# Second attention on one Trainium2 core: q and k in two float32r parts instead of three bf16 parts, heads of even and odd number on separate partition halves

## The chip, the core and the metric

The kernel runs on one core of a Trainium2 chip. A core has a matrix engine (TensorE, in the views PE for its matmuls and PEld for the loading of their stationary operands), a vector engine (DVE), an engine for activations (ACT), a general one (POOL) and one that issues transfers (SP). They run side by side and wait for each other with semaphores. The metric is the device time of one execution in microseconds, lower is better; the time of a version is the median of its runs.

## The reference

Two layers are computed on 2048 tokens of 128 features: a windowed attention, a memory layer, a second attention and a layer of experts, each behind a layer norm. The change is in the second attention: 16 heads of width 8 over one sequence of N = 2048.

```python
def _L1_attn_ref(x, Wq, bq, Wk, bk, Wv, bv, Wo, bo):
    ...
    q = (x @ Wq.T + bq).reshape(B, N, H, d).transpose(0, 2, 1, 3)
    k = (x @ Wk.T + bk).reshape(B, N, H, d).transpose(0, 2, 1, 3)
    v = (x @ Wv.T + bv).reshape(B, N, H, d).transpose(0, 2, 1, 3)
    q, k = _rope(q, k)
    scores = jnp.einsum('bhnd,bhmd->bhnm', q, k) / jnp.sqrt(jnp.asarray(d, x.dtype))
    attn = jax.nn.softmax(scores, axis=-1)
    out = jnp.einsum('bhnm,bhmd->bhnd', attn, v)
```

## The kernel before

The kernel is written engine by engine, with every wait by hand. Four stages take nearly all the time: the first attention (until about 400 us of the span), the memory layer (until about 480), the second attention with its projections (482 to 1376), and the experts (the last 90 us).

`project1_block` makes q and k with their rotation, 512 columns at a time in eight jobs, and splits each float32 value into three bf16 parts whose sum is the value. DVE rotates and takes the first rest, ACT rounds, POOL takes the last rest (line 847), and SP stores the parts to device memory.

`attn1_block` then works through the 16 heads. For one head, all scores of a query with 2048 keys are needed twice:

- **R**, the row-maximum matmuls (`rows`, line 973): queries on the output's partitions, keys along the free axis, 64 matmuls of 128 by 512 per head. DVE takes the maximum of 1024 columns at a time (line 1055), so 32 reductions per head.
- **E**, the exponential's matmuls (line 1019): keys on the partitions, queries along the free axis, again 64 of 128 by 512. The maximum of each query is subtracted inside the matmul by extra contraction rows, which hold the negated maxima in parts. ACT takes the exponential of each (line 1127).
- **AV** (`weigh`, line 999): values and a column of ones, in float32, weighted by the exponentials. The four blocks of 512 queries stand side by side on four strips of 32 columns of the array. A float32 matmul is two instructions in the views.

A head has 16 *slots* t of 128 keys (numbered 0 to 15 here). In slot t, TensorE issues four E, E0 to E3, with R of a later head between them, and then AV of slot t - 1. Each E waits for a free bank: two banks hold scores for ACT, so E2 waits for the exponential of E0 and E3 for that of E1. R starts 12 matmuls ahead (`LEAD`), so in slots 0 to 12 R belongs to head h + 1 and in slots 13 to 15 to head h + 2. At the end of slot 13 `turn_max` (line 982) turns the maxima of the next head, DVE copies them (line 1076), and SP writes them into the contraction rows. After slot 15 DVE copies the sums (line 1082), TensorE turns them, and DVE divides.

Heads 0 to 11 run in a hardware loop of four rounds with three heads each; heads 12 to 15 are written out. Between E the loop places R by this line:

```python
for c, beside in enumerate((1, 2, 1, 0)):
```

so nothing stands between E3 and AV. q and k of a head are one tile of 72 or 75 partitions (three parts times three parts times eight, and three rows for the maximum).

Of the kernel before, what the change touches and what calls it, by code (L numbers as in the profile page):

```python
# [6 lines left out]
F32 = mybir.dt.float32  # L7
BF16 = mybir.dt.bfloat16
U32 = mybir.dt.uint32
ACT = mybir.ActivationFunctionType  # L10
ALU = mybir.AluOpType
# [23 lines left out]
PARTS = 3  # L35
QROWS = PARTS * PARTS * HD1
MROW = QROWS
KROWS = QROWS + PARTS
VCOLS = 32
# [717 lines left out]
def project1_block(nc, m, a):  # L757

    with ExitStack() as ctx:
# [9 lines left out]
        rot = sb("rot", [P, 2, BANK])  # L769
        rest = sb("rest", [P, 2, BANK])  # L770
        parts = sb("parts", [P, 2, PARTS, N], BF16)

        swapped = sem("swapped")
        qk_ready, partner_ready = sem("qk_ready"), sem("partner_ready")
        rot_ready, part1, rest_ready, part2, part3 = sem("rot_ready"), sem("part1"), sem("rest_ready"), sem("part2"), sem("part3")
# [28 lines left out]
        def _(dve):  # L804
# [5 lines left out]
            for s in range(JOBS + 1):  # L810
                if s < JOBS:
                    u, i, c = s, s // NC, s % NC
                    dve.wait_ge(qk_ready, u + 1)
                    if u >= 2:
                        dve.wait_ge(rot_ready, u - 1)
                    cols = slice(c * BANK, (c + 1) * BANK)
                    nc.vector.scalar_tensor_tensor(direct[:, u % 2, :], m.psum[:, 2 * (u % 3), :], biases[i][:, 0:1],
                                                   m.cos[:, cols], ALU.add, ALU.mult)
                    nc.vector.scalar_tensor_tensor(partner[:, u % 2, :], m.psum[:, 2 * (u % 3) + 1, :], biases_sw[i][:, 0:1],
                                                   m.sin[:, cols], ALU.add, ALU.mult).then_inc(partner_ready, 1)  # L820
                u = s - 1
                if u >= 0:
                    i, c = u // NC, u % NC
                    dve.wait_ge(rot_ready, u + 1)
                    dve.wait_ge(part1, u + 1)
                    if u >= 2:
                        dve.wait_ge(part3, u - 1)
                    nc.vector.tensor_tensor(rest[:, u % 2, :], rot[:, u % 2, :], parts[:, i, 0, c * BANK:(c + 1) * BANK],
                                            ALU.subtract).then_inc(rest_ready, 1)
                if s < JOBS:  # L830
                    dve.wait_ge(partner_ready, s + 1)
                    if s >= 2:
                        dve.wait_ge(rest_ready, s - 1)
                    nc.vector.tensor_tensor(rot[:, s % 2, :], direct[:, s % 2, :], partner[:, s % 2, :], ALU.add).then_inc(rot_ready, 1)
# [5 lines left out]

        @block.gpsimd
        def _(pool):
            for u in range(JOBS):
                i, c = u // NC, u % NC
                pool.wait_ge(part2, u + 1)
                cols = slice(c * BANK, (c + 1) * BANK)
                nc.gpsimd.tensor_tensor(parts[:, i, 2, cols], rest[:, u % 2, :], parts[:, i, 1, cols], ALU.subtract).then_inc(part3, 1)

        @block.scalar
        def _(act):  # L850
            for s in range(JOBS + 1):
                if s < JOBS:
                    i, c = s // NC, s % NC
                    act.wait_ge(rot_ready, s + 1)
                    nc.scalar.activation(parts[:, i, 0, c * BANK:(c + 1) * BANK], rot[:, s % 2, :], ACT.Copy).then_inc(part1, 1)
                u = s - 1
                if u >= 0:
                    i, c = u // NC, u % NC
                    act.wait_ge(rest_ready, u + 1)
                    nc.scalar.activation(parts[:, i, 1, c * BANK:(c + 1) * BANK], rest[:, u % 2, :], ACT.Copy).then_inc(part2, 1)  # L860

        @block.sync
        def _(sp):
            for u in range(JOBS):
                i, c = u // NC, u % NC
                cols = slice(c * BANK, (c + 1) * BANK)
                sp.wait_ge(part3, u + 1)

                sp.dma_start((m.q_parts, m.k_parts)[i].rearrange("s r n -> r s n")[:, :, cols], parts[:, i, :, cols]).then_inc(stored, 16)
            sp.wait_ge(stored, 16 * JOBS)  # L870


def attn1_block(nc, m, a):

    SCALE = HD1 ** -0.5
    HALF = 2 * BANK  # L880
    NB = 3
    with ExitStack() as ctx:
# [6 lines left out]
        qf = sb("qf", [KROWS, NB, N], BF16)  # L889
        kf = sb("kf", [KROWS, NB, N], BF16)  # L890
        vx = sb("vx", [P, NB, NT, VCOLS])
        pb = sb("pb", [P, 2, NC, BANK])
        rowmax = sb("rowmax", [P, NT, 2])
        nmax = sb("nmax1", [P, NT])
        nrest = sb("nrest", [P, NT])
        nparts = sb("nparts", [P, P // NT, NT], BF16)
        nT = sb("nT", [PARTS * NT, P], BF16)
# [3 lines left out]
        loaded = [sem(f"qk_loaded{b}") for b in range(NB)]  # L901
        ones_loaded = sem("ones_loaded")
        nparts_zeroed = sem("nparts_zeroed")
        vx_zeroed, vx_ready = sem("vx_zeroed"), sem("vx_ready")
        rows_ready, rows_reduced = sem("rows_ready"), sem("rows_reduced")
        nmax_ready, npart1, nrest1, npart2, npart3 = sem("nmax_ready"), sem("npart1"), sem("nrest1"), sem("npart2"), sem("npart3")
# [5 lines left out]

        START = 2

        def start_counts(eng, *sems):
            for s in sems:
                eng.sem_inc(s, START)


# [3 lines left out]
        ROUNDS = H1 // NB - 1  # L923
        LEAD = 12
        LOAD = 16 * 2 * PARTS

# [5 lines left out]
        def _(sp):  # L932
            def load(h, b):
# [7 lines left out]
            def max_rows(g, b):  # L941

                sp.wait_ge(nT_saved, START + g + 1)
                sp.dma_start(qf[QROWS:KROWS, b, :], nT[:, :]).then_inc(max_rows_loaded, 16)

            for b in range(NB):
                load(b, b)
                if b == 0:
                    sp.dma_start(kf[QROWS:KROWS, :, :], m.ones_rows.rearrange("r (o n) -> r o n", o=1)
                                 .broadcast_to([PARTS, NB, N])).then_inc(ones_loaded, 16)  # L950
            max_rows(0, 0)
            with sp.Fori(0, ROUNDS) as r:
                for b in range(NB):
                    max_rows(r * NB + b + 1, (b + 1) % NB)

                    sp.wait_ge(av_done, START + (r * NB + b + 1) * NT)
                    load(r * NB + b + NB, b)
            for h in range(H1 - 1 - NB, H1 - 1):
                max_rows(h + 1, (h + 1) % NB)
                if h == H1 - 1 - NB:  # L960
                    sp.wait_ge(av_done, START + (h + 1) * NT)
                    load(h + NB, h % NB)
# [538 lines left out]
```

## Time and profile before

| what | value |
|---|---|
| median of 3 runs | 1500.69 us (1499.51 to 1502.81) |
| span of the profiled execution | 1493.4 us |
| its mean granted TensorE clock | 0.939 of full speed |
| TensorE busy | 1353.5 us (91%) |
| DVE busy | 1035.1 us (69%) |
| ACT busy | 916.2 us (61%) |
| POOL busy | 173.4 us (12%) |

The span runs from the first to the last instruction. The profiled execution has no separate time of its own beside it; the median of the runs is 7.3 us above its span, and this is taken as what lies around the span. Busy shares are averages over stages with different limits, and a busy TensorE is not one at its peak.

### The profile page before, as it was taken

Reading aid. Unit: us, or ns where it says so; the run is one execution under the profiler, and the core shown is the slowest. Engines: PE = TensorE matmul, PEld = TensorE weight load, DVE = VectorE, ACT = ScalarE, POOL = GpSimd, SP = SyncE. Lnnn points to the kernel's source line nnn. Section 1 sums busy time; section 2 is a strip of 40 time slices with the busy share of each in tenths; the row PEclk is TensorE's granted clock in tenths of the full one; section 3 lists DMA queues with packets and bytes.
Section 4 is the critical chain, followed back from the end, with each engine's and each line's share of the span. In section 5 each row is a group of like instructions: output and inputs, shape, how many; then the busy total and the mean of one; then the engine's idle time right before and its main releaser. Section 6 shows DMA issues by size and latency. Waiting matters only on the chain. (4 is left out here: it accounts for less than half of the span.)

```text
span 1493.4 us, 24477 instructions
## 1 busy us (share of the span) xinstructions
PE 1353.5 (91%) x7460; PEld 605.9 (41%) x7460; DVE 1035.1 (69%) x1993; ACT 916.2 (61%) x2409; POOL 173.4 (12%) x321
## 2 busy tenths in 40 slices
PE   4999999999787669999899989998999999999698
PEld 2676776777545301222222222222222222223466
DVE  4677777777768678888677877887788887750400
ACT  2666666666565303776577667666766676668442
POOL 3233222333320500000000000000000000001200
PEclk8899999999989755999799989999999999999799
DMA  3100000000000210000000000000000000000200
GB/s 84 49 8 9 5 2 8 7 2 1 1 1 1 87 46 1 5 13 17 18 1 17 17 18 1 17 17 11 8 17 17 2 16 17 1 1 1 49 0 28
DMA packets 21889, 23.33 MB, mean 16 GB/s; under 512 B 5640, under 2 KB 18184, under 8 KB 21522
## 3 DMA queue, kind: packets, MB, share of 16 engines
q1 hardware_dynamic: 21778, 21.94, 4.5%
q8 instruction: 58, 0.95, 0.3%
q14 instruction: 53, 0.43, 0.1%
HBM read 17.54 MB, written 4.19 MB: 15 GB/s over the span
## 5 line engine op out<-in xcount | busy, mean ns | idle before, releaser
L1127 ACT ACTIVATE pb<-psum 128x512 f32<-128x512 f32 x1024 | 554.1, 595 | 288.3 <-PE psum L1019 287.6
L1055 DVE TENSOR_REDUCE rowmax<-psum 128x1 f32<-128x1024 f32 x512 | 602.9, 1219 | 147.7 <-PE psum L973 147.2
L1019 PE MATMUL psum<-qf,kf 75*128 75x512 bf16 x1024 | 395.0, 394 | 14.6 <-issue 10.0
L973 PE MATMUL psum<-kf,qf 72*128 72x512 bf16 x1024 | 374.8, 408 | 31.2 <-DVE rowmax L1055 16.7
L999 PE MATMUL psum<-pb,vx 128*32 128x512 f32 x2048 | 274.8, 614 | 0.6 <-ACT pb L1127 0.6
L1019 PEld LDWEIGHTS psum<-qf,kf 75*128 75x128 bf16 x1024 | 99.2, 98 | 391.0 <-ACT pb L1127 331.1
L490 ACT ACTIVATE pr<-sm,nmax 128x128 f32<-128x128 f32 x256 | 100.7, 394 | 104.6 <-DVE nmax L429 101.9
L973 PEld LDWEIGHTS psum<-kf,qf 72*128 72x128 bf16 x1024 | 99.6, 100 | 137.7 <-DVE rowmax L1055 63.5
L527 POOL TENSOR_TENSOR pr<-pr,rtotal 128x256 f32<-128x256 f32 (+1 forms) x256 | 110.5, 453 | 262.9 <-DVE rtotal L437 262.9
L424 DVE TENSOR_TENSOR sm<-psum,mask 128x320 f32<-128x320 f32 x128 | 62.2, 486 | 48.4 <-PE psum L298 48.4
L298 PE MATMUL psum<-kx,qz 128*128 128x160 f32 x512 | 92.1, 303 | 0.0
L298 PEld LDWEIGHTS psum<-kx,qz 128*128 128x128 f32 x512 | 79.0, 193 | 28.0 <-issue 27.7
L1144 POOL COPY vx<-v 128x128 f32 (+1 forms) x16 | 4.6, 293 | 716.6 <-PE psum L999 716.6
L492 ACT ACTIVATE pr<-sm,nmax 128x32 f32<-128x32 f32 x256 | 78.3, 306 | 0.0
L999 PEld LDWEIGHTS psum<-pb,vx 128*32 128x32 f32 x2048 | 42.0, 108 | 73.8 <-issue 61.5
L338 PE MATMUL psum<-wo_cur,oT 128*128 128x128 f32 x256 | 62.8, 327 | 0.2
L325 PE MATMUL psum<-pt,gv 64*128 64x128 f32 x256 | 62.7, 325 | 0.0
L1323 ACT ACTIVATE hT<-psum,b 128x512 f32<-128x512 f32 x48 | 33.0, 687 | 43.2 <-PE psum L1338 43.0
L428 DVE TENSOR_REDUCE nmax<-sm 128x2 f32<-128x256 f32 x128 | 53.8, 420 | 4.4
L327 PE MATMUL psum<-pt,v 128*64 128x128 f32 x512 | 56.7, 300 | 0.0
L312 PE MATMUL psum<-ident,pr 128*128 128x128 f32 x256 | 51.0, 281 | 5.6 <-POOL pr L527 4.4
L443 DVE COPY pt<-psum 128x256 f32<-128x256 f32 x128 | 50.8, 397 | 1.5 <-PE psum L314 1.3
(198 smaller groups left out, 1337.7 us busy)
## 6 DMA issues: line engine op xcount, KB each, us to landing
qf<-q_parts SPq DMA_DIRECT2D x48, 96.0 KB
kf<-k_parts SPq DMA_DIRECT2D x48, 96.0 KB
q_parts<-parts SPq DMA_DIRECT2D x4, 384.0 KB, 2.5
k_parts<-parts SPq DMA_DIRECT2D x4, 384.0 KB, 2.5
cos<-cos_table SPq DMA_DIRECT2D x1, 1024.0 KB, 5.2
sin<-sin_table SPq DMA_DIRECT2D x1, 1024.0 KB, 7.0
out<-x SPq DMA_DIRECT2D x1, 1024.0 KB, 5.1
w_cur<-in_L_attn_wq SPq DMA_DIRECT2D x8, 64.0 KB, 1.9
```

Of the source, the lines that this page charges most:

```text
L298: mm = nc.tensor.matmul(m.psum[:, S_B + i % 2, j * WL:(j + 1) * WL], qz[:, b, j, s * P:(s + 1) * P], kx[:, b, s, :], start=True, stop=True)
L325: nc.tensor.matmul(ob, gv[:, b, :], pt[0:2 * G0, w % 2, 2 * P:3 * P], start=True, stop=False)
L338: nc.tensor.matmul(m.psum[:, Y_B, (w % TPB) * P:(w % TPB + 1) * P], oT[:, w % 4, :], wo_cur[:, b, :], start=True, stop=True).then_inc(wo_d ...
L424: nc.vector.tensor_tensor(sm[:, i % 4, :], m.psum[:, S_B + i % 2, 0:2 * WL], m.mask[:, :], ALU.add).then_inc(masked, 1)
L490: nc.scalar.activation(pr[:, i % 4, j * P:(j + 1) * P], sm[:, i % 4, j * WL:j * WL + P], ACT.Exp, bias=nmax[:, i % 4, j:j + 1], accum_out= ...
L492: mm = nc.scalar.activation(pr[:, i % 4, 2 * P + j * G0:2 * P + (j + 1) * G0], sm[:, i % 4, j * WL + P:(j + 1) * WL], ACT.Exp, bias=nmax[: ...
L527: mm = nc.gpsimd.tensor_tensor(prw, prw, rb, ALU.mult)
L973: mm = nc.tensor.matmul(m.psum[:, M_B + (u % 2) * 2 + n % 2, :], qf[0:QROWS, b, t * P:(t + 1) * P], kf[0:QROWS, b, c * BANK:(c + 1) * BANK ...
L999: mm = nc.tensor.matmul(m.psum[c * VCOLS:(c + 1) * VCOLS, A_B, :], vx[:, b, t, :], pb[:, t % 2, c, :], start=(t == 0), stop=(t == NT - 1))
L1019: nc.tensor.matmul(m.psum[:, bank, :], kf[:, b, t * P:(t + 1) * P], qf[:, b, c * BANK:(c + 1) * BANK], start=True, stop=True).then_inc(st_ ...
L1055: nc.vector.tensor_reduce(rowmax[:, u // 2, u % 2:u % 2 + 1], m.psum[:, M_B + (u % 2) * 2:M_B + (u % 2) * 2 + 2, :].rearrange("p b c -> p ...
L1127: nc.scalar.activation(pb[:, t % 2, c, :], m.psum[:, exp_bank(k, last)[0], :], ACT.Exp, scale=SCALE).then_inc(exp_ready, 1)
```

## The change

q and k are split into two float32r parts instead of three bf16 parts. (float32r is a float32 of which the matrix engine uses a shortened mantissa.) A head then needs 33 contraction rows for R and 35 for E: even heads are held on partitions 0 to 63, odd ones on 64 to 127. E of head h and R of head h + 1 lie on different halves of the array's rows. The order on TensorE becomes one R behind each E, and all 16 heads are written out. In `project1_block` DVE and ACT each lose a step of the split, and POOL's now reads the rotated value itself. On DVE the split of the maxima falls away; it is done behind the transpose, in two steps instead of one copy. POOL fills the constant rows, which a transfer did before.

```diff
-PARTS = 3
-QROWS = PARTS * PARTS * HD1
-MROW = QROWS
+PARTS = 2
+PROWS = PARTS * PARTS * HD1
+QROWS = PROWS + 1
 KROWS = QROWS + PARTS
+HALFP = P // 2
 VCOLS = 32
...
-                    nc.vector.tensor_tensor(rest[:, u % 2, :], rot[:, u % 2, :], parts[:, i, 0, c * BANK:(c + 1) * BANK],
-                                            ALU.subtract).then_inc(rest_ready, 1)
...
+                nc.scalar.activation(parts[:, i, 0, c * BANK:(c + 1) * BANK], rot[:, u % 3, :], ACT.Copy).then_inc(high_ready, 1)
...
+                nc.gpsimd.tensor_tensor(parts[:, i, 1, cols], rot[:, u % 3, :], parts[:, i, 0, cols].bitcast(F32),
+                                        ALU.subtract).then_inc(low_ready, 1)
...
-        qf = sb("qf", [KROWS, NB, N], BF16)
-        kf = sb("kf", [KROWS, NB, N], BF16)
+        qf = sb("qf", [P, SLOTS, N], F32R)
+        kf = sb("kf", [P, SLOTS, N], F32R)
...
+        def group(h):
+            return h % 2 * HALFP
+        def slot(h):
+            return h // 2 % SLOTS
...
+            def load(h):
+                g0, b = group(h), slot(h)
+                hd = slice(h * HD1, (h + 1) * HD1)
                 for j in range(PARTS):
-                    rows = slice(j * PARTS * HD1, (j + 1) * PARTS * HD1)
-                    k = m.k_parts[j, bass.ds(h * HD1, HD1), :].rearrange("(o d) n -> o d n", o=1)
-                    sp.dma_start(qf[rows, b, :], m.q_parts[:, bass.ds(h * HD1, HD1), :]).then_inc(loaded[b], 16)
-                    sp.dma_start(kf[rows, b, :], k.broadcast_to([PARTS, HD1, N])).then_inc(loaded[b], 16)
+                    part = slice(g0 + j * PARTS * HD1, g0 + (j + 1) * PARTS * HD1)
+                    q = m.q_parts[j, hd, :].rearrange("(o d) n -> o d n", o=1).broadcast_to([PARTS, HD1, N])
+                    sp.dma_start(qf[part, b, :].bitcast(F32), q).then_inc(loaded[h % 4], 16)
+                    sp.dma_start(kf[part, b, :].bitcast(F32), m.k_parts[:, hd, :]).then_inc(loaded[h % 4], 16)
+            def max_rows(h):
+                g0, b = group(h), slot(h)
+                sp.wait_ge(nT_saved, h + 1)
+                sp.dma_start(qf[g0 + QROWS:g0 + QROWS + 1, b, :].bitcast(F32), nT[0:NT, :].bitcast(F32)).then_inc(max_rows_loaded, 16)
+                sp.dma_start(qf[g0 + QROWS + 1:g0 + KROWS, b, :].bitcast(F32), nT[HALFP // 2:HALFP // 2 + NT, :].bitcast(F32)).then_inc(max_rows_loaded, 16)
...
+            def rows(g, n):
                 t, c, u = n // NC, n % NC, n // 2
-                if n % 2 == 0:
-                    pe.wait_ge(rows_reduced, START + g * HALVES + u - 1)
-                mm = nc.tensor.matmul(m.psum[:, M_B + (u % 2) * 2 + n % 2, :], qf[0:QROWS, b, t * P:(t + 1) * P],
-                                      kf[0:QROWS, b, c * BANK:(c + 1) * BANK], start=True, stop=True)
+                g0, b = group(g), slot(g)
+                if n % 2 == 0 and g * HALVES + u >= 2:
+                    pe.wait_ge(rows_reduced, g * HALVES + u - 1)
+                mm = nc.tensor.matmul(m.psum[:, M_B + (u % 2) * 2 + n % 2, :], qf[g0:g0 + QROWS, b, t * P:(t + 1) * P],
+                                      kf[g0:g0 + QROWS, b, c * BANK:(c + 1) * BANK], start=True, stop=True)
...
+                nc.tensor.transpose(m.psum[0:2 * NT, T_B, 0:P], nmax[:, :], m.ident[:, :]).then_inc(nT_ready, 1)
...
+            def head(h):
+                g0, b = group(h), slot(h)
+                left = H1 - 1 - h
+                pe.wait_ge(max_rows_loaded, (h + 1) * 32)
                 n = LEAD
                 for t in range(NT + 1):
                     if n == UNITS and left >= 2:
-                        b2 = b + 2
-                        pe.wait_ge(loaded[b2 % NB], r * LOAD + (1 + b2 // NB) * LOAD)
-                    for c, beside in enumerate((1, 2, 1, 0)):
+                        pe.wait_ge(loaded[(h + 2) % 4], ((h + 2) // 4 + 1) * LOAD)
+                    for c in range(NC):
                         if t == NT:
                             break
                         k = t * NC + c
                         bank, banks = exp_bank(k, left == 0)
-                        pe.wait_ge(exp_ready, START + h * UNITS + k + 1 - banks)
-                        nc.tensor.matmul(m.psum[:, bank, :], kf[:, b, t * P:(t + 1) * P],
-                                         qf[:, b, c * BANK:(c + 1) * BANK], start=True, stop=True).then_inc(st_ready, 1)
-                        for _ in range(beside):
-                            if n < UNITS and left >= 1:
-                                rows(h + 1, (b + 1) % NB, n)
-                            elif n >= UNITS and left >= 2:
-                                rows(h + 2, (b + 2) % NB, n - UNITS)
-                            n += 1
+                        if h * UNITS + k + 1 - banks > 0:
+                            pe.wait_ge(exp_ready, h * UNITS + k + 1 - banks)
+                        nc.tensor.matmul(m.psum[:, bank, :], kf[g0:g0 + KROWS, b, t * P:(t + 1) * P],
+                                         qf[g0:g0 + KROWS, b, c * BANK:(c + 1) * BANK], start=True, stop=True).then_inc(st_ready, 1)
+                        if n < UNITS and left >= 1:
+                            rows(h + 1, n)
+                        elif n >= UNITS and left >= 2:
+                            rows(h + 2, n - UNITS)
+                        n += 1
...
+            for h in range(H1):
+                head(h)
...
-            def split_maxima(g):
-                dve.wait_ge(rows_reduced, START + (g + 1) * HALVES)
-                nc.vector.tensor_reduce(nmax[:, :], rowmax[:, :, :], AX_X, ALU.max, negate=True).then_inc(nmax_ready, 1)
-                nc.vector.tensor_copy(nparts[:, 0, :], nmax[:, :]).then_inc(npart1, 1)
-                nc.vector.tensor_tensor(nrest[:, :], nmax[:, :], nparts[:, 0, :], ALU.subtract).then_inc(nrest1, 1)
-                nc.vector.tensor_copy(nparts[:, 1, :], nrest[:, :]).then_inc(npart2, 1)
-                nc.vector.tensor_tensor(nparts[:, 2, :], nrest[:, :], nparts[:, 1, :], ALU.subtract).then_inc(npart3, 1)
+            def save_maxima(g):
+                dve.wait_ge(rows_reduced, (g + 1) * HALVES)
+                nc.vector.tensor_reduce(nmax[:, 0:NT], rowmax[:, g % 2, :, :], AX_X, ALU.max, negate=True).then_inc(nmax_ready, 1)
...
+                nc.vector.tensor_copy(nT[0:NT, :], m.psum[0:NT, T_B, 0:P]).then_inc(nhigh_ready, 1)
+                dve.wait_ge(nhigh_ready, g + 1)
+                nc.vector.tensor_tensor(nT[HALFP // 2:HALFP // 2 + NT, :], m.psum[0:NT, T_B, 0:P], nT[0:NT, :].bitcast(F32),
+                                        ALU.subtract).then_inc(nT_saved, 1)
...
+            for h in range(H1):
                 for k in range(UNITS):
                     t, c = k // NC, k % NC
...
+            for i, g0 in enumerate((0, HALFP)):
+                if i:
+                    pool.wait_ge(edge_rows, 2)
+                nc.gpsimd.memset(qf[g0 + PROWS:g0 + QROWS, :, :].bitcast(F32), 0.0).then_inc(edge_rows, 1)
+                pool.wait_ge(edge_rows, 2 * i + 1)
```

In TensorE's order, here in slot 1 of head 0 (L1019 is E, L973 is R, L999 is AV, the rows of registers are the loop's counts), before:

```order
615 L1019 MATMUL psum<-qf,kf 128x512
616 L972 REGISTER_ALU
617 L973 MATMUL psum<-kf,qf 128x512
618 L1018 REGISTER_ALU
619 L1019 MATMUL psum<-qf,kf 128x512
620 L973 MATMUL psum<-kf,qf 128x512
621 L972 REGISTER_ALU
622 L973 MATMUL psum<-kf,qf 128x512
623 L1018 REGISTER_ALU
624 L1019 MATMUL psum<-qf,kf 128x512
625 L973 MATMUL psum<-kf,qf 128x512
626 L1018 REGISTER_ALU
```

and behind those the fourth E and AV at once:

```order
627 L1019 MATMUL psum<-qf,kf 128x512
628 L999 MATMUL psum<-pb,vx 32x512 x4
629 L1018 REGISTER_ALU
630 L1019 MATMUL psum<-qf,kf 128x512
```

In the changed program the same slot (L992 is E, L945 is R, L972 is AV):

```order
598 L992 MATMUL psum<-qf,kf 128x512
599 L945 MATMUL psum<-kf,qf 128x512
600 L992 MATMUL psum<-qf,kf 128x512
601 L945 MATMUL psum<-kf,qf 128x512
602 L992 MATMUL psum<-qf,kf 128x512
603 L945 MATMUL psum<-kf,qf 128x512
604 L992 MATMUL psum<-qf,kf 128x512
605 L945 MATMUL psum<-kf,qf 128x512
606 L972 MATMUL psum<-pb,vx 32x512 x4
607 L992 MATMUL psum<-qf,kf 128x512
```

The last R has moved from ahead of E3 to between E3 and AV.

On DVE, around the maxima of head 1, before (L1055 is the reduction of R's scores):

```order
746 L1062 TENSOR_REDUCE nmax<-rowmax 128x16
747 L1063 REGISTER_ALU
748 L1064 CAST nparts<-nmax 128x16
749 L1066 TENSOR_TENSOR nrest<-nmax,nparts 128x16
750 L1068 CAST nparts<-nrest 128x16
751 L1070 TENSOR_TENSOR nparts<-nrest,nparts 128x16
752 L1054 REGISTER_ALU
753 L1055 TENSOR_REDUCE rowmax<-psum 128x1
754 L1074 REGISTER_ALU
755 L1076 COPY nT<-psum 48x128
```

and in the changed program (L1023 is the reduction, L1036 and L1038 write the turned maxima):

```order
681 L1030 TENSOR_REDUCE nmax<-rowmax 128x16
682 L1023 TENSOR_REDUCE rowmax<-psum 128x1
683 L1036 CAST nT<-psum 16x128
684 L1038 TENSOR_TENSOR nT<-psum,nT 16x128
685 L1023 TENSOR_REDUCE rowmax<-psum 128x1 x5
```

Four short steps ahead of the transpose are gone, and one has come behind it.

## Rows read from the trace of the kernel before

**Rows 1.** Groups by line: shapes, count | busy us, mean ns | idle before, releaser.

```profile
L1127 ACT ACTIVATE pb<-psum 128x512 f32<-128x512 f32 x1024 | 554.1, 595 | 288.3 <-PE psum L1019 287.6
...
L1055 DVE TENSOR_REDUCE rowmax<-psum 128x1 f32<-128x1024 f32 x512 | 602.9, 1219 | 147.7 <-PE psum L973 147.2
...
L1019 PE MATMUL psum<-qf,kf 75*128 75x512 bf16 x1024 | 395.0, 394 | 14.6 <-issue 10.0 <-ACT pb L1127 3.9
...
L973 PE MATMUL psum<-kf,qf 72*128 72x512 bf16 x1024 | 374.8, 408 | 31.2 <-DVE rowmax L1055 16.7 <-DMA kf<-ones_rows 12.9
```

**Rows 2.** Timeline, one slot of head 4: start us, length us, engine, line.

```profile
802.65 0.39 PE L1019 MATMUL psum<-qf,kf 75*128 75x512 bf16 x1
802.88 0.38 PE L973 MATMUL psum<-kf,qf 72*128 72x512 bf16 x1
...
803.08 2.17 ACT L1127 ACTIVATE pb<-psum 128x512 f32<-128x512 f32 x4 [0.71 <-PE psum L1019]
...
804.22 0.39 PE L1019 MATMUL psum<-qf,kf 75*128 75x512 bf16 x1
804.53 1.07 PE L999 MATMUL psum<-pb,vx 128*32 128x512 f32 x8
805.53 0.39 PE L1019 MATMUL psum<-qf,kf 75*128 75x512 bf16 x1
```

**Rows 3.** Timeline, head 14, slots without row-maximum matmuls.

```profile
1335.82 1.06 PE L999 MATMUL psum<-pb,vx 128*32 128x512 f32 x8
...
1338.77 1.49 PE L999 MATMUL psum<-pb,vx 128*32 128x512 f32 x12
```

**Rows 4.** Timeline, head 12, unrolled, with row-maximum matmuls.

```profile
1215.83 1.06 PE L999 MATMUL psum<-pb,vx 128*32 128x512 f32 x8
...
1218.77 1.07 PE L999 MATMUL psum<-pb,vx 128*32 128x512 f32 x8
```

**Rows 5.** Timeline of TensorE in the first attention.

```profile
302.38 0.38 PE L312 MATMUL psum<-ident,pr 128*128 128x128 f32 x2
302.60 0.27 PE L314 MATMUL psum<-ident,pr 128*64 128x128 f32 x1
302.80 0.49 PE L325 MATMUL psum<-pt,gv 64*128 64x128 f32 x2
```

**Rows 6.** Timeline, slot 14 of head 7.

```profile
982.73 0.22 DVE L1076 COPY nT<-psum 48x128 bf16<-48x128 bf16 x1 [0.58 <-PE psum L982]
...
984.14 0.39 PE L973 MATMUL psum<-kf,qf 72*128 72x512 bf16 x1 [0.76 <-DVE rowmax L1055]
```

**Rows 7.** Timeline: accumulator copies after heads 2, 3, 4; first matmul of head 3.

```profile
728.75 0.69 DVE L1082 COPY acc<-psum 128x512 f32<-128x512 f32 x1 [0.44 <-PE psum L999]
...
733.41 0.61 PE L1019 MATMUL psum<-qf,kf 75*128 75x512 bf16 x1 [3.26 <-issue]
...
787.30 0.69 DVE L1082 COPY acc<-psum 128x512 f32<-128x512 f32 x1 [0.44 <-PE psum L999]
...
836.32 0.69 DVE L1082 COPY acc<-psum 128x512 f32<-128x512 f32 x1 [0.44 <-PE psum L999]
```

**Rows 8.** One stretch: length, busy PE, PEld, DVE, ACT, POOL (count), PEclk (0.50: 1.2 GHz), DMA, GB/s.

```profile
577.00:591.00 14.00, 14.00 (x41) 3.33 (x39) 8.75 (x8) 7.05 (x12) 0.00 (x0) 0.50 0.00 0
```

**Rows 9.** Timeline, head 0, one slot at the low clock.

```profile
583.91 1.93 PE L999 MATMUL psum<-pb,vx 128*32 128x512 f32 x8
...
585.78 0.61 PE L1019 MATMUL psum<-qf,kf 75*128 75x512 bf16 x1
...
586.42 0.60 ACT L1127 ACTIVATE pb<-psum 128x512 f32<-128x512 f32 x1 [1.80 <-PE psum L1019]
...
589.30 1.94 PE L999 MATMUL psum<-pb,vx 128*32 128x512 f32 x8
```

**Rows 10.** Groups by line: one POOL step of the split, one memset.

```profile
L847 POOL TENSOR_TENSOR parts<-rest,parts 128x512 bf16<-128x512 f32 x8 | 16.3, 2048 | 12.2 <-ACT parts L860 12.2
...
L1138 POOL MEMSET vx<- 128x1536 f32 x1 | 1.4, 1377 | 3.4 <-POOLq L759 3.4
```

More of the change, by code:

```diff
@@ L8 @@
 BF16 = mybir.dt.bfloat16
+F32R = mybir.dt.float32r
 U32 = mybir.dt.uint32
@@ L839, in _ @@
                                         m.psum[:, 6 + c % 2, :].rearrange("p (t d) -> p t d", d=D), bv, ALU.add).then_inc(v_saved, 1)
+        @block.scalar
+        def _(act):
+            for u in range(JOBS):
+                i, c = u // NC, u % NC
+                act.wait_ge(rot_ready, u + 1)
+                nc.scalar.activation(parts[:, i, 0, c * BANK:(c + 1) * BANK], rot[:, u % 3, :], ACT.Copy).then_inc(high_ready, 1)
         @block.gpsimd
@@ L844, in _ @@
                 i, c = u // NC, u % NC
-                pool.wait_ge(part2, u + 1)
+                pool.wait_ge(high_ready, u + 1)
                 cols = slice(c * BANK, (c + 1) * BANK)
[L847 to L860, printed above, removed]
+                nc.gpsimd.tensor_tensor(parts[:, i, 1, cols], rot[:, u % 3, :], parts[:, i, 0, cols].bitcast(F32),
+                                        ALU.subtract).then_inc(low_ready, 1)
         @block.sync
@@ L941, in max_rows @@
[L941 to L957, printed above, removed]
@@ L1040, in _ @@
                     turn_max(0)
-                rows(1, 1, n)
-            with pe.Fori(0, ROUNDS) as r:
-                for b in range(NB):
-                    head(r, b)
-            for h in range(ROUNDS * NB, H1):
-                head(h // NB, h % NB)
+                rows(1, n)
+            for h in range(H1):
+                head(h)
         @block.vector
         def _(dve):
-            start_counts(dve, rows_reduced, nmax_ready, npart1, nrest1, npart2, npart3, nT_saved, acc_saved, rsum_ready, att_ready)
@@ L1089, in sums, with maxima @@
                 nc.vector.tensor_tensor(dst, turned[:, :, :, 0:HD1], rb, ALU.mult).then_inc(att_ready, 1)
[L1091 to L1097 removed]
+            def maxima(g):
+                save_maxima(g)
+                if g + 1 < H1:
                     reduce_rows(g + 1, 0, 1)
                 save_turned(g)
[L1100 removed]
+                if g + 1 < H1:
@@ L1101, in maxima @@
                     reduce_rows(g + 1, 1, LEAD // 2)
+            nc.vector.memset(nmax[:, NT:2 * NT], 0.0).then_inc(nmax_zeroed, 1)
+            dve.wait_ge(nmax_zeroed, 1)
             reduce_rows(0, 0, HALVES)
-            maxima(0, True)
-            with dve.Fori(0, ROUNDS) as r:
-                for b in range(NB):
-                    h = r * NB + b
-                    reduce_rows(h + 1, LEAD // 2, HALVES)
-                    maxima(h + 1, True)
-                    sums(h)
-            for h in range(ROUNDS * NB, H1):
+            maxima(0)
```

197 lines of the change are left out of this document (78 added, 119 removed).

## Prediction

> **What bounds the kernel now.** I read the groups by line first, then the timeline of one slot. In the second attention every engine has much to do: ACT 1024 exponentials of 595 ns, DVE 512 reductions of 1219 ns, TensorE 1024 E and 1024 R [rows 1]. Per slot (256 of them) that is 2.4 us of DVE and 2.2 us of ACT. The idle columns matter more: ACT sat idle 287.6 us waiting for E, while TensorE seems never to be idle. That looks like a kernel bound by TensorE, and putting E and R beside each other then looks like a gain of up to 0.4 us a slot, down to DVE's 2.44.
>
> The timeline says otherwise. One slot goes from the E0 at 802.65 to that at 805.53, 2.88 us. It is a chain: E0 to its exponential 0.43 (802.65 to 803.08), two exponentials until E3 may write into the freed bank 1.14 (to 804.22), E3 to AV 0.31 (804.53), AV to the next E0 1.00 (805.53); together 2.88 [rows 2]. R is not in it: R fills gaps. The proof is in head 14, whose last slots have no R at all: AV to AV is still 2.95 us there [rows 3], against 2.94 us in head 12 with four R per slot [rows 4]. So taking R off TensorE's time is worth nothing by itself. What counts is what the change does to the four links of this chain.
>
> The unrolled heads also show a price: 2.94 [rows 4] against 2.88 us in the loop [rows 2]. The loop's ends show another: copy to copy, head 3 takes 58.55 us (728.75 to 787.30), head 4 49.02 (to 836.32); head 3's first matmul came only at 733.41 after 3.26 us of "issue" [rows 7]. The ends of rounds two and three cost 6.8 us each by the same copies (55.8 and 55.7 us), the first 9.5.
>
> **The change part by part.**
>
> *E and R side by side.* As the chain has no R, 0 us in slots 0 to 12, if the halves do run together. The cover is that R3, now between E3 and AV, costs nothing there. Without it R3 adds the step from one matmul to the next, 0.23 us from 802.65 to 802.88 [rows 2]; I take 0.22.
>
> *Loading the stationary operand.* E3 waits for ACT and E0 follows AV, so their weights can't be loaded ahead; the load lies open in the chain twice per slot. For bf16 it shows as almost nothing: the step behind E0 is the same 0.23 [rows 2], hardly more than 512 columns at 2.4 GHz, 0.21. For a four-byte operand the nearest row is the float32 pair at 302.80: two matmuls of 64 rows by 128 columns take 0.49 us together where a pair of transposes takes 0.38, so the open load costs 0.11; the 0.20 from 302.60 to 302.80 against a step of 0.11 is the price of changing the array's shape, 0.09 [rows 5]. That price is paid around AV today as well. Bounds for the load: 0 (as bf16) and 0.11 (as float32). I take 0.10, because float32r has the same 4 bytes and 128 columns, on half the rows, as that row. Thus +0.20 us in each of 13 slots of 15 heads: +39 us.
>
> The Trainium skill, TensorE: Matmul & The Clock Gate, section on weight-path perf modes, says that the fast weight load is on for 128 weights when the dtype is not FP32. Read to the letter, float32r could be fast, which is the first rival below (1494 us); by its other statement, that reading 32 bits at a time brings no win for fp32, the sum stays.
>
> *Slots 13 to 15.* Here R belongs to head h + 2, on the same half as E, so nothing can overlap, and R3 stands in the chain: +0.22, and twice the load, +0.20, in slots 13 and 15. That is 2 x 0.42 x 14 heads = +12 us. Slot 14 is held by DVE today: R waits until 984.14 for a reduction that stood behind the copy at 982.73 [rows 6]. The four short steps that go lay ahead of the transpose, in time in which DVE waited 0.58 us for it anyway; the second step behind it adds some 0.2 us, and E3, still behind R2, is no earlier by more than that. +0.1 x 14 = +1.5 us; bounds -3 and +5.
>
> *Head ends and the last head.* E0 behind the transposes meets a change of shape and an open load, 0.2 x 15 = +3. The last head has no R and four banks; one open load per slot, +1.5.
>
> *Unrolling.* +0.06 us per slot in the 12 heads of the loop, some 14 slots each: +10 us. The ends of the rounds go: 9.5 + 6.8 + 6.8 = -23 us, with the low clock behind them.
>
> *Projections and start.* DVE loses a step, and POOL, with 8 steps of 2048 ns and 12.2 us of idle time in between and before, then sets the pace; each job may get some 0.3 us shorter, -2 to -3. Before the first R, POOL now writes four constant tiles of 4096 columns; at 1377 ns for 1536 columns [rows 10] each takes some 3.5 us, 14 in all, where TensorE waited 12.9 us for the transfer that goes [rows 1]. Nothing to +1. Together -3, bounds -4 and +1. SP issues two transfers for the maxima instead of one, with slots 14 and 15 to hide them before the next head; loads for head h + 4 are queued behind them and are not needed for a whole head. Nothing.
>
> Sum: 39 + 12 + 1.5 + 3 + 1.5 + 10 - 23 - 3 = +41. On the profiled span of 1493.4 that is 1534, and with 7.3 us around the span **1542 us**.
>
> **The rivals.**
>
> *The load is hidden or short (27%).* Then 39 and 1.5 fall away, slots 13 and 15 cost 6, head ends 1.5: -7 us, 1494. At half the price, 1518. For it: that bf16 pays nothing. Against: [rows 5]. This is the rival on the other side; it decides when the open load is under 0.015 us. A version of it in which something in the chain also shortens would go to 1480.
>
> *The low clock spreads (26%).* From 577 to 591, in head 0, TensorE was busy without a gap (14.00 of 14.00 us), E and R with 75 and 72 rows, and the granted clock stayed at 0.50, that is 1.2 GHz [rows 8]. So full busy time did not bring it back at once. The changed kernel does less on TensorE per slot: four pairs and AV are about 1.9 us of 3.1, and from a head's last AV to the first of the next pass some 6 us (an estimate: copy and transposes, then slots 0 and 1). If the clock falls there and does not return before the next end, slots cost what they would at 1.2 GHz. Today such a slot takes 5.39 us (583.91 to 589.30); its AV alone 1.87, E0 to ACT 0.64 [rows 9]. With pairs: 1.87 + 0.8 + 1.14 (ACT does not slow down) + 0.6 = 4.4 to 4.6, so +1.4 over my 3.1. For all 15 heads with their slower ends that is some +350: 1890. If only three slots per head run so, +60: 1600. For it: the work is on 68 rows in two halves, where 75 rows did not suffice. Against: in the loop the clock fell only behind a wait like that of 3.26 us [rows 7], and its mean over the span was 0.939. The same page (Part 1, the HAM clock gate) says that the granted clock has two levels only, half and full; the trace shows no other.
>
> *No overlap (8%).* R3 in the chain of all slots: 0.22 x 13 x 15 = +43 more, 1585. The skill, TensorEngine Tiling (Array Packing), section on key properties, says that tiles run loads and matmuls in parallel. What shows it in this trace is only the four column strips of AV: eight instructions of 614 ns in 1.06 us [rows 2].
>
> *float32r streams its columns twice (5%)*, as each instruction of a float32 pair does: +0.21 in E0 and in E3, about +0.43 x 240 slots = +105: 1645.
>
> *Something shortens the chain (4%)*: 1450 to 1490.
>
> **How the numbers follow.** The forecast itself has 30%, with a range of its own from 1525 to 1560. The likeliest single case is the point, not a mean. Faster by over 0.2% (about what a measurement of this kernel can tell from no change) comes from five sixths of the first rival and the last one, 25%; no change from a price between, 5%; slower from the rest, 70%. The range leaves out the best tenth and the worst: 1487, just under the hidden load, to 1870, just under an attention wholly at the low clock.
>
> **What would show it.** In the changed profile: slots 2 to 12 at 3.14 us from AV to AV, with 0.41 from E3 to AV and 0.53 from E0 to ACT (the load); E and R of a pair starting together; slots 13 and 15 at 3.3 to 3.4; equal head lengths with no "issue" wait of 3 us; granted clock near 1. A slot of 2.94 says that the load was hidden, 3.36 that nothing overlapped, 4.5 with PEclk 0.50 that the clock fell. I am wrong in kind if slots come under 2.88: then TensorE's time did bound, and the slots of head 14 misled me.

## The result and the profile after

The changed kernel takes 1936.2 us (median of 4 runs, 1935.9 to 1938.2), where the kernel before takes 1500.1: the ratio is 1.290, interval 1.288 to 1.292. I had predicted 1542 with a range up to 1870. The profiled execution spans 1933.2 us, 439.8 more than before.

The page of the changed kernel shows where to look (busy tenths in 40 slices, and the granted clock below them):

```profile
PE 1756.5 (91%) x7460; PEld 804.0 (42%) x7460; DVE 1053.8 (55%) x1937; ACT 918.9 (48%) x2398; POOL 181.3 (9%) x325
...
PE   4999999978489999999999999999999999999798
...
PEclk9999999999755555555555555555555555555699
```

DVE and ACT do nearly as much as before in microseconds, but their shares of the longer span have sunk. TensorE looks busy nearly all the time, yet from the eleventh or twelfth slice to the last ones its granted clock is 0.50, that is 1.2 GHz. The groups by line answer to [rows 1]:

```profile
L1082 ACT ACTIVATE pb<-psum 128x512 f32<-128x512 f32 x1024 | 564.8, 596 | 727.4 <-PE psum L992 725.8
L1023 DVE TENSOR_REDUCE rowmax<-psum 128x1 f32<-128x1024 f32 x512 | 625.4, 1225 | 478.1 <-PE psum L945 475.3
L992 PE MATMUL psum<-qf,kf 35*128 35x512 f32 x1024 | 635.4, 703 | 65.1 <-ACT pb L1082 64.7
L945 PE MATMUL psum<-kf,qf 33*128 33x512 f32 x1024 | 630.9, 698 | 19.6 <-POOL kf L1093 15.3
...
L972 PE MATMUL psum<-pb,vx 128*32 128x512 f32 x2048 | 490.5, 1058 | 0.0
```

An exponential takes what it took, but ACT now waits 726 us for E (288 before [rows 1]). AV, which the change did not touch, takes 1058 ns an instruction. One slot of the changed kernel in the timeline (start us, length us), against [rows 2]:

```profile
1003.43 0.79 PE L992 MATMUL psum<-qf,kf 35*128 35x512 f32 x1
...
1003.44 0.79 PE L945 MATMUL psum<-kf,qf 33*128 33x512 f32 x1
...
1004.03 0.62 PE L992 MATMUL psum<-qf,kf 35*128 35x512 f32 x1
1004.03 0.62 PE L945 MATMUL psum<-kf,qf 33*128 33x512 f32 x1
1004.32 1.09 ACT L1082 ACTIVATE pb<-psum 128x512 f32<-128x512 f32 x2 [2.05 <-PE psum L992]
...
1005.56 0.69 PE L992 MATMUL psum<-qf,kf 35*128 35x512 f32 x1
...
1006.18 1.93 PE L972 MATMUL psum<-pb,vx 128*32 128x512 f32 x8
...
1008.05 0.79 PE L992 MATMUL psum<-qf,kf 35*128 35x512 f32 x1
```

The edit does what it says: E and R of a pair start within 0.01 us of each other. But the chain is longer at each link that runs on TensorE: E0 to its exponential 0.89 (0.43 before), E3 to AV 0.62 (0.31), AV to the next E0 1.87 (1.00). Between the exponential and E3, two exponentials on ACT, it is nearly the old one, 1.24 (1.14). Together 4.62 us instead of 2.88. Three stretches of the same trace (length, busy PE, PEld, DVE, ACT, POOL, PEclk, DMA, GB/s) show that the clock stays there:

```profile
612.00:656.00 44.00, 42.09 (x145) 15.46 (x145) 22.23 (x21) 20.19 (x36) 0.00 (x0) 0.50 0.00 1
656.00:662.00 6.00, 4.67 (x28) 1.60 (x20) 3.03 (x5) 1.33 (x3) 0.29 (x1) 0.78 0.04 11
662.00:735.00 73.00, 69.23 (x247) 23.62 (x249) 38.71 (x34) 34.22 (x62) 0.00 (x0) 0.50 0.02 7
```

In head 0 TensorE is busy for 42.09 of 44 us and has the low clock. Only around the end of some heads, behind a slot 15 in which it did AV after AV on all 128 rows, does the full clock come for a few microseconds (the 0.78), and it is gone again within slot 0 of the next head. The accumulator copies, one per head, give the sum. The first row is of the changed kernel, the second of the kernel before (durations, then first and last start):

```profile
L1046 DVE COPY acc<-psum x16: 691/692/692, 658.4 to 1815.2; 128x512 f32<-128x512 f32 x16
```

```profile
L1082 DVE COPY acc<-psum x16: 691/692/692, 630.6 to 1375.2; 128x512 f32<-128x512 f32 x16
```

The first copy is 27.8 us later; the 15 intervals up to the last copy take 1156.8 instead of 744.6 us, +412.2; behind it nothing differs. 27.8 + 412.2 = 440.0, the whole difference of the spans (439.8). All of the loss lies in the second attention and its start: 27.5 us for each interval on the average, and 29 against a head of the loop that has no end of a round (78.1 against 49.0).

### The profile page after: what moved, and what is told of

It is laid out like the page before. It is cut to its first block and busy times, and to the rows that moved or that the text cites. A ratio compares the mean times of both kernels' runs of the same rounds, so it can differ in the third digit from the quotient of the medians.

```text
span 1933.2 us, 21772 instructions
## 1 busy us (share of the span) xinstructions
PE 1756.5 (91%) x7460; PEld 804.0 (42%) x7460; DVE 1053.8 (55%) x1937; ACT 918.9 (48%) x2398; POOL 181.3 (9%) x325
## 5 line engine op out<-in xcount | busy, mean ns | idle before, releaser
L1082 ACT ACTIVATE pb<-psum 128x512 f32<-128x512 f32 x1024 | 564.8, 596 | 727.4 <-PE psum L992 725.8
L1023 DVE TENSOR_REDUCE rowmax<-psum 128x1 f32<-128x1024 f32 x512 | 625.4, 1225 | 478.1 <-PE psum L945 475.3
L992 PE MATMUL psum<-qf,kf 35*128 35x512 f32 x1024 | 635.4, 703 | 65.1 <-ACT pb L1082 64.7
L945 PE MATMUL psum<-kf,qf 33*128 33x512 f32 x1024 | 630.9, 698 | 19.6 <-POOL kf L1093 15.3
L992 PEld LDWEIGHTS psum<-qf,kf 35*128 35x128 f32 x1024 | 276.8, 293 | 625.9 <-issue 330.6
L972 PE MATMUL psum<-pb,vx 128*32 128x512 f32 x2048 | 490.5, 1058 | 0.0
L945 PEld LDWEIGHTS psum<-kf,qf 33*128 33x128 f32 x1024 | 278.4, 297 | 58.3 <-DVE rowmax L1023 31.8
L972 PEld LDWEIGHTS psum<-pb,vx 128*32 128x32 f32 x2048 | 54.6, 142 | 137.7 <-issue 89.8
L1102 POOL COPY vx<-v 128x128 f32<-128x128 f32 x16 | 4.6, 293 | 1060.4 <-PE psum L972 1060.4
L1046 DVE COPY acc<-psum 128x512 f32<-128x512 f32 x16 | 11.1, 692 | 103.4 <-PE psum L972 103.4
```

The lines of the kernel that those rows point to most:

```text
L945: mm = nc.tensor.matmul(m.psum[:, M_B + (u % 2) * 2 + n % 2, :], qf[g0:g0 + QROWS, b, t * P:(t + 1) * P], kf[g0:g0 + QROWS, b, c * BANK:(c ...
L972: mm = nc.tensor.matmul(m.psum[c * VCOLS:(c + 1) * VCOLS, A_B, :], vx[:, h % VB, t, :], pb[:, t % 2, c, :], start=(t == 0), stop=(t == NT ...
L992: nc.tensor.matmul(m.psum[:, bank, :], kf[g0:g0 + KROWS, b, t * P:(t + 1) * P], qf[g0:g0 + KROWS, b, c * BANK:(c + 1) * BANK], start=True, ...
L1023: nc.vector.tensor_reduce(rowmax[:, g % 2, u // 2, u % 2:u % 2 + 1], m.psum[:, M_B + (u % 2) * 2:M_B + (u % 2) * 2 + 2, :].rearrange("p b ...
L1082: nc.scalar.activation(pb[:, t % 2, c, :], m.psum[:, exp_bank(k, h == H1 - 1)[0], :], ACT.Exp, scale=SCALE).then_inc(exp_ready, 1)
```

## The experiments

My theory was now: TensorE lacks not busy time but rows. E contracts over 35 rows and R over 33, and the clock does not come back at that. The rivals: float32r with its open loads keeps it down; or the longer chain does; or that two matmuls run beside each other.

### Fill up the rows, change nothing else

```diff
-QROWS = PROWS + 1
-KROWS = QROWS + PARTS
+QROWS = 64 - PARTS
+KROWS = 64
```

> The changed kernel, with the operands of E and R filled up with rows that add nothing (zero in q): E contracts over 64 rows instead of 35, R over 62 instead of 33; no instruction is added. Theory (the clock stays at 1.2 GHz because the two halves together use 68 of 128 rows): the granted clock is 1.00 in slots 2 to 12, a slot takes 3.1 us instead of 4.61, and the time is 1520 to 1560 us. Rival (float32r, its loads that lie open or the longer waits of the chain keep the clock down, whatever the rows): clock 0.50, slot 4.6 us, 1936 us.

Measured: 1614.9 us (median of three runs, 1606.3 to 1624.7; a fourth took 1636.1), ratio 1.078 (1.071 to 1.084), mean clock 0.898 instead of 0.661. The four times follow their mean clocks: 0.900, 0.898, 0.892 and 0.880 from the fastest to the slowest. It is 321 us faster than the changed kernel with not one instruction more: only rows that add nothing (zeros in q) are contracted over as well. A slot in the timeline of head 9, which has the full clock:

```profile
1139.57 0.50 PE L992 MATMUL psum<-qf,kf 64*128 64x512 f32 x1
1139.57 0.50 PE L945 MATMUL psum<-kf,qf 62*128 62x512 f32 x1
1139.91 0.39 PE L992 MATMUL psum<-qf,kf 64*128 64x512 f32 x1
...
1140.17 2.27 ACT L1082 ACTIVATE pb<-psum 128x512 f32<-128x512 f32 x4 [0.88 <-PE psum L992]
...
1141.30 0.49 PE L992 MATMUL psum<-qf,kf 64*128 64x512 f32 x1
...
1141.73 1.07 PE L972 MATMUL psum<-pb,vx 128*32 128x512 f32 x8
1142.72 0.50 PE L992 MATMUL psum<-qf,kf 64*128 64x512 f32 x1
```

The slot is 3.15 us (1139.57 to 1142.72), as expected. The time missed my 1520 to 1560, because the clock is still lost at most heads' ends. Three stretches of head 1, from its middle, from the start of slot 13 until the clock fell, and behind that:

```profile
655.00:684.00 29.00, 24.90 (x150) 8.19 (x152) 22.27 (x20) 20.15 (x38) 0.00 (x0) 1.00 0.00 1
681.40:688.20 6.80, 6.38 (x33) 3.00 (x33) 4.74 (x8) 4.21 (x8) 0.00 (x0) 1.00 0.02 5
689.00:697.00 8.00, 8.00 (x28) 2.99 (x24) 2.76 (x3) 2.39 (x4) 0.00 (x0) 0.50 0.00 0
```

What TensorE did before it fell: slots 13 and 14, in which R belongs to the head after next, on the same half as E. There E and R, 64 and 62 rows, run one after the other and no longer together. In those 6.80 us TensorE was busy for a larger share (94%, with one gap of 0.34 us) than in the stretch before (86%), where the clock stayed full; after 689 it was busy for 8.00 of 8.00 us and had half the clock. In ten of the first fourteen heads the clock falls in slot 14. A head that starts without it takes 61.7 us from copy to copy (697.1 to 758.8). Heads 9 to 11 lose it only in slot 1, for 3.4 us, and take 54.7 to 54.9, here the interval up to the copy of head 10:

```profile
1170.45 0.69 DVE L1046 COPY acc<-psum 128x512 f32<-128x512 f32 x1 [0.66 <-PE psum L972]
...
1225.19 0.69 DVE L1046 COPY acc<-psum 128x512 f32<-128x512 f32 x1 [0.66 <-PE psum L972]
```

### Few rows in the kernel before

```diff
-kf[:, b, t * P:(t + 1) * P], qf[:, b, c * BANK:(c + 1) * BANK]
+kf[64:KROWS, b, t * P:(t + 1) * P], qf[64:KROWS, b, c * BANK:(c + 1) * BANK]
-qf[0:QROWS, b, t * P:(t + 1) * P], kf[0:QROWS, b, c * BANK:(c + 1) * BANK]
+qf[64:QROWS, b, t * P:(t + 1) * P], kf[64:QROWS, b, c * BANK:(c + 1) * BANK]
```

> The kernel before, with nothing changed but the rows that E and R contract over: E 11 instead of 75 (one product of parts and the three rows of the maximum), R 8 instead of 72; so the scores are only a part of what they should be, and the instructions, their order and their bf16 are those of before. Theory (rows): the clock falls to 0.50 at the first head and stays there; each slot costs what a slot of before costs at that clock, 5.39 instead of 2.88 us, so about 256 x 2.5 = +640, some 2140 us. Rival (float32r or the new chain, not the rows): 1500 us, clock full.

Measured: 2069.7 us (one run), mean clock 0.645. Slots 2 to 12 take 5.39 us in each head but the last:

```profile
601.81 0.60 PE L1019 MATMUL psum<-qf,kf 11*128 11x512 bf16 x1
...
607.20 0.60 PE L1019 MATMUL psum<-qf,kf 11*128 11x512 bf16 x1
```

```profile
600.00:650.00 50.00, 50.00 (x153) 10.96 (x152) 22.56 (x23) 22.09 (x37) 0.00 (x0) 0.50 0.00 1
```

TensorE is busy for 50.00 of 50.00 us at the clock of 0.50. That is the slot that the kernel before has only in slots 1 and 2 after a stop [rows 9]. Bf16, the loop, the old order, no side by side, and the loss is there, so neither float32r nor the new order nor the running together is needed for it. The experiment before has all three of them, and with more rows its clock is mostly full. The values in this kernel differ too, as its scores are partial; that can't be the cause there, where only rows that add nothing came in. My +640 came out as +571, because slots 0 and the head ends, and the last head, grow less than a middle slot.

### Heads written out

```diff
-            with pe.Fori(0, ROUNDS) as r:
+            for r in range(ROUNDS):
```

(and likewise on the other four engines)

> The kernel before with the heads of the second attention written out on every engine and nothing else. My terms: the three ends of rounds go (-9.5 - 6.8 - 6.8 = -23 us), and slots of unrolled heads cost 0.06 us more (+10): 1487 us, 0.991 of before. Rival a (instructions that are written out cost TensorE nothing): 1477. Rival b (the code of unrolled heads has to be fetched, and waits of 3 us come back at other places): 1500 or more.

Measured: 1483.1 us, ratio 0.989 (0.987 to 0.992); once more beside another kernel below, 1483.3. The unrolled half of the change, taken alone, is a gain. A slot:

```profile
860.18 0.39 PE L1019 MATMUL psum<-qf,kf 75*128 75x512 bf16 x1
860.50 1.06 PE L999 MATMUL psum<-pb,vx 128*32 128x512 f32 x8
861.50 0.39 PE L1019 MATMUL psum<-qf,kf 75*128 75x512 bf16 x1
...
861.99 1.68 ACT L1127 ACTIVATE pb<-psum 128x512 f32<-128x512 f32 x3 [0.78 <-PE psum L1019]
...
863.13 0.39 PE L1019 MATMUL psum<-qf,kf 75*128 75x512 bf16 x1
```

The 0.06 us that written-out heads cost lies in the first link: E0 to its exponential 0.49, in the loop 0.43; the other links are as in [rows 2]. The long ends of rounds [rows 7] are gone: every head of the former loop takes 49.7 to 50.0 us.

### All heads on one half

```diff
-            return h % 2 * HALFP
+            return 0
-            return h // 2 % SLOTS
+            return h % SLOTS
-        SLOTS = 2
+        SLOTS = 4
```

> The changed kernel with every head on partitions 0-63, so that E and R use the same rows and cannot run beside each other; operands, order and rows (35 and 33) as in the changed kernel. Theory (rows): clock 0.50 as in the changed kernel, and R, which at that clock has no gap left to fill, adds its own streaming to the slot: 4.61 + 3 x 0.43 or 4 x 0.43 = 5.9 to 6.3 us, in all 1936 + 15 x 13 x 1.5 = some 2230 us. Rival (it is the running beside each other that holds the clock down): clock near 1 as before, slots of 3.1 to 3.4 us, 1540 to 1600. Second rival (in the changed kernel E and R did not truly overlap at the low clock): 1936.

Measured: 2125.1 us (one run), clock 0.642. A slot from E0 to E0:

```profile
1079.84 0.79 PE L992 MATMUL psum<-qf,kf 35*128 35x512 f32 x1
1080.43 0.62 PE L945 MATMUL psum<-kf,qf 33*128 33x512 f32 x1
...
1083.55 1.93 PE L972 MATMUL psum<-pb,vx 128*32 128x512 f32 x8
1085.41 0.79 PE L992 MATMUL psum<-qf,kf 35*128 35x512 f32 x1
```

5.57 us, less than my 5.9 to 6.3, since in the changed kernel TensorE still had 0.5 us in which to wait for ACT (E1 at 1004.03, E2 at 1004.97, with one stream of 0.43 between), and part of R went there. So at 1.2 GHz, where TensorE with E and R in series bounds the slot, running side by side saves 5.57 - 4.62 = 0.95 us a slot. It does not cause the low clock; it softens it.

### Float32r alone, with all 128 rows

```diff
-QROWS = PROWS + 1
-KROWS = QROWS + PARTS
+QROWS = P - PARTS
+KROWS = P
-                    for c in range(NC):
+                    for c, beside in enumerate((1, 2, 1, 0)):
```

(on top of the kernel with all heads on one half; each E is followed by `beside` calls of `rows`)

> Float32r without running side by side: every head on the same partitions, E and R filled up with rows of zeros to 128 and 126, and R3 back in its place of before (after E1). What is left of the change is the operand type with its open loads, and the unrolled heads. My step on the load: slots of 2.94 + 2 x 0.10 = 3.15 us (2.94 as in the unrolled kernel of before); clock 1.00, the head ends as in the unrolled kernel before; 1483 + 195 x 0.21 + slots 13 to 15 and head ends (some 4) = 1525 to 1535 us. If E and R beside each other is worth nothing at the full clock, the slot is the same 3.15 as in the filled-up changed kernel, where they do run side by side. Rival (side by side hides part of the streams or of the loads): slots over 3.15, up to 3.36.

Measured: 1553.2 us, ratio 1.037 (1.034 to 1.040). Slots, E0 to E0:

```profile
874.87 0.50 PE L992 MATMUL psum<-qf,kf 128*128 128x512 f32 x1
875.21 0.40 PE L945 MATMUL psum<-kf,qf 126*128 126x512 f32 x1
...
878.02 0.50 PE L992 MATMUL psum<-qf,kf 128*128 128x512 f32 x1
```

3.15 us, heads of 53.4. The total is some 20 us above what I expected, and not by these slots: POOL writes the constant rows of q and k for four heads now instead of two, which holds up the first R to 545.7 us (531.4 before), 14 us. It is the columns that count there and not the rows of zeros: with 35 and 33 rows on one half the first R comes at 545.3. The rest is that slot 14 takes 4.37 us instead of the 3.65 of the unrolled kernel, 0.7 us in 14 heads, 10 us. What it tells: float32r in series and float32r side by side have the same slot at the full clock, so **the side-by-side edit is worth nothing there**, as the chain said; and the operand type costs 3.15 - 2.94 = 0.21 us, two open loads of 0.10 as forecast.

### R3 behind E3 in bf16

```diff
-                    for c, beside in enumerate((1, 2, 1, 0)):
+                    for c, beside in enumerate((1, 1, 1, 1)):
```

> The unrolled kernel of before with R3 between E3 and AV, where the change has it, in bf16 and in series: the price of that place when nothing overlaps. My step: 0.22 us a slot, 2.94 to 3.16 us; 1483 + 0.22 x 13 x 15 + slots 13 and 15 (2 x 0.22 x 14 = 6) = some 1532 us. Rival (the chain of E0, the exponentials and E3 leaves time elsewhere): less.

Measured: 1516.4 us (one run); E3 to AV grows from 0.32 to 0.54:

```profile
800.98 0.39 PE L1019 MATMUL psum<-qf,kf 75*128 75x512 bf16 x1
801.21 0.38 PE L973 MATMUL psum<-kf,qf 72*128 72x512 bf16 x1
801.52 1.06 PE L999 MATMUL psum<-pb,vx 128*32 128x512 f32 x8
```

The slot has my 3.16 us. The total is 16 below my 1532, since slots 0, 1 and 14 do not become longer (heads of 52.2 us, where 0.22 in each of 15 slots would give 53.0), and since the first E came 3.8 us earlier in this run (573.6 against 577.4). So in the changed kernel side by side only takes back what its own order would have cost, and no more.

### More rows in the kernel before

```diff
-KROWS = QROWS + PARTS
+KROWS = P
+MAXR = KROWS - PARTS
-qf[QROWS:KROWS, b, :], nT
+qf[MAXR:KROWS, b, :], nT
-qf[0:QROWS, b, t
+qf[0:MAXR, b, t
```

(and for kf; zeros are written into rows 64 to 127 first)

> The kernel before, loop and all, with E and R filled up with rows of zeros (E 128, R 125 instead of 75 and 72). Theory (rows bring the clock back sooner): the slots of 5.39 us that follow a wait at heads 0, 3, 6 and 9 (two and a bit in each) become one or none, up to 4 x 6 = -24 us, some -12 to -22; plus 1 to 3 us for writing the zeros ahead of the first load: 1480 to 1492 us. Rival (rows count only as on or off, 75 rows do what 128 do): 1500 to 1503.

> The unrolled kernel of before (1483) with the same rows of zeros. Only head 0 has slots at the low clock there (3.96, 5.39, 5.39 us): theory (rows) -3 to -5 us and +1 to +3 for the zeros: 1479 to 1484. The float terms of two theories are close here; it is run because it may be the fastest, and to see if the slot itself (2.94 us) stays untouched by rows.

Measured: the loop 1486.9, ratio 0.992 (0.989 to 0.994); the unrolled one 1483.5, ratio 0.991 (0.988 to 0.993), no better than without the rows. Both lie where the theory had them. In the loop the intervals with an end of a round fall from 55.7 to 58.6 us to 53.5 to 54.1, and the others stay at some 48.9, so 128 rows do more than 75. In both the first E comes 6 to 9 us later behind the zeros, more than the 1 to 3 that I gave them. Last, the zeros of the first head written first:

```diff
-                nc.vector.memset(qf[64:P, :, :], 0.0)
+                for b in range(NB): nc.vector.memset(qf[64:P, b, :], 0.0)
```

(likewise kf; only the third load of a head waits for them)

> The unrolled kernel of before with rows of zeros, and the zeros of the first head written first (1024 to 2048 columns at a time) so that the first loads do not wait for all of them. In the filled-up unrolled kernel the first E came 6 us later than in the one without zeros (583.6 against 577.4), and that ate what the three slots of head 0 gave back. If the zeros of one head cost under 2 us, 1478 to 1481 us, against 1483 for the unrolled kernel alone; if the later zeros still hold up the loads of heads 1 and 2, 1483.

> The unrolled kernel of before once more, on the same chip as the filled-up one, for a difference of a few microseconds: 1483.

Measured: 1478.5, ratio 0.986 (0.983 to 0.989), and 1483.3, 0.989 (0.986 to 0.991). The first is the fastest version that I found. The two intervals against the kernel before overlap, but the times themselves do not (1477.0 to 1480.9 against 1481.5 to 1483.9, on the same chip), and the profiles show the gain in head 0. The same 17 us in head 0, for E and R with 11 and 8 rows, with 75 and 72 rows (unrolled), and with 128 and 125 rows, each a row of its own trace:

```profile
583.00:600.00 17.00, 17.00 (x55) 3.66 (x56) 8.14 (x8) 7.76 (x13) 0.00 (x0) 0.50 0.00 0
```

```profile
583.00:600.00 17.00, 17.00 (x71) 4.08 (x69) 10.49 (x9) 9.84 (x18) 0.00 (x0) 0.73 0.00 0
```

```profile
583.00:600.00 17.00, 17.00 (x92) 4.50 (x96) 13.76 (x13) 13.04 (x25) 0.00 (x0) 1.00 0.00 0
```

TensorE is busy for 17.00 of 17.00 us in all three; the granted clock is 0.50, 0.73 and 1.00 (the 0.73 is a mean over a stretch at 0.50 and one at 1.00). The number of matmuls that get done follows it: 55, 71, 92.

## Why the prediction was wrong

**What bounds the kernel**: right. The slot is the chain that I had read, link by link; R is not in it. With the full clock, both halves together and R in series, in its place of before, give the same 3.15 us.

**The failed step is the clock.** The sum of my forecast has no term for it: I took as likeliest (30%) that the clock stays near full, and gave "The low clock spreads" 26%. The evidence stood in [rows 8]: TensorE busy without a gap, E and R with 75 and 72 rows, and the clock at 0.50 for 14 us. I read it as a delay before the clock comes back ("full busy time did not bring it back at once") and as a matter of pauses ("in the loop the clock fell only behind a wait"). The experiments show that it was a matter of rows: with 75 and 72 rows in series, or 64 and 62 side by side, the clock is back two to three slots into the head, with 128 and 125 within the first, and with 35 and 33 side by side not in a whole head. So the mechanism that I had written down for the rival, few rows, is the one that ruled, but a quarter was too little for it: the change halves the rows of every E and R, in the very place where the trace showed the clock hesitating. The term that I had put at nothing measured 1936 less some 1547 us (the sum at the full clock, below), about 390.

The Trainium skill, TensorE: Matmul & The Clock Gate (Part 1, the HAM clock gate), says that the clock follows how busy TensorE has been and that it has two levels. On the levels the trace agrees: stretches inside a head show 0.50 or 1.00. On busy time, as the profile counts it, it does not: 17.00 of 17.00 us is busy in the row at 0.50 as in that at 1.00; the measurement decides.

**The rival's size**: slots at 4.4 to 4.6, measured 4.62. Its total of 1890 is 46 short. I had left out the last head, which takes 62.5 us copy to copy at the low clock and 37.0 with 64 rows; another 5 is the start (below), and the rest is slots 13 to 15, which at that clock take 5.9, 5.6 and 8.8 to 9.2 us. My range ended at 1870 because it was cut just under this very case; the measured time lies 66 us beyond it.

**The load**: right in size. 2 x 0.10 forecast, 0.21 measured in two experiments; float32r does not stream twice (E0 to E1 is 0.34 us, 1139.57 to 1139.91: one stream of 0.23 and the load). So the first rival (hidden load, 1494) and the one of two streams (1645) are both refuted, as is "no overlap".

**Slots 13 to 15 and head ends**: right in the sum. My terms give heads of 53.5 us. The heads of 54.7 in the filled-up kernel hold 1.2 us from the 3.4 us at the low clock: slot 1 takes 4.03 and slot 2 3.46 there, against 3.16 and 3.15 in head 8, whose clock is full in both. Without it they too take 53.5; the float32r kernel in series has 53.4. The parts are less even: slot 13 took 3.60 where I had 3.43, slot 14 some 3.97 where I had 3.75, and slot 1 took less.

**Unrolling**: right in size. -23 + 10 = -13 forecast; measured 1498.9 to 1483.1 on the same chip, -16, and -13 in the spans of the two profiles.

**Projections and start**: I had -3. The first R comes at 533.3, 1.9 us later than before (531.4), so the sign was wrong, by some 5 us. (The first E is 4.2 us later; the stretch between the two runs at the low clock in both kernels.) The step of POOL, which I had kept at 2048 ns, came to 1266.

**Two slips that change nothing**: five sixths of 27% and 4% are 26 to 27%, where I wrote 25%. And the 7.3 us do not lie around the span: every later run has its time 1.7 to 2.9 us above its span. The rest is the spread of the executions, 1491.4 to 1504.3 us for this kernel over all runs. In the sum the 7.3 only lifts the base to the median.

At the full clock, then, the sum would have been 1542 + 5 = some 1547, an estimate. No run has this exactly: the kernel with 64 rows a half comes to 1614.9 because it loses the clock at most head ends. How the time would stand if it kept it there was not tried.

## What to carry to other kernels

Before you narrow a matmul's contraction (fewer parts, packing two on half the array each), look for the stretches in which TensorE is busy and its granted clock is still 0.50: there busy time alone does not bring the clock back, and fewer rows can lose it for good. A chain with AV and E in it then pays at every link. If such a kernel is slow, compare granted clocks before anything else, and try rows of zeros: they cost no instruction in the loop, only their writing at the start. In the filled-up changed kernel even that was free (first E at 580.8 us, 581.1 without), since POOL writes constant rows there anyway; in the kernel before it cost 6 to 9 us until it was put in a better order. And taking work off an engine that looks 90% busy is worth nothing while it only fills gaps of a chain; its exact place in the order (R3 behind E3, 0.22 us) is worth more.

## What the runs showed of the hardware that I had not expected

- Rows of zeros count: filling E and R from 35 and 33 to 64 and 62 rows with zeros brought the mean clock from 0.661 to 0.898.
- The clock can be lost while TensorE is busy nearly all the time: in the filled-up kernel it fell in slot 14 of head 1, behind 6.80 us in which TensorE was busy for 6.38 us with E and R one after the other on 64 and 62 rows.
- What POOL takes to write constant rows follows the columns and not the rows: 6.92 us for 8192 columns on one row as on 32 (all heads on one half), 3.50 us for 4096 (changed kernel).
- A float32r load of the stationary operand takes 183 ns (median at the full clock), and one of bf16 98; in the chain the difference shows as 0.11 us for each load that lies open. It hardly depends on rows: at the full clock it takes 183 ns with 35 as with 64 rows, and 186 to 190 with 126 and 128. The rows are loads of R in the kernel before and in the one with 126 rows (min, median, max in ns):

```profile
L973 PEld LDWEIGHTS psum<-kf,qf x1024: 95/98/152, 531.4 to 1329.1; 72*128 72x128 bf16 x171
```

```profile
L945 PEld LDWEIGHTS psum<-kf,qf x1024: 186/190/339, 545.7 to 1382.6; 126*128 126x128 f32 x171
```
